# Second cross attention: ScalarE rounds the tokens, and the order of token and key work changes

## The reference

```
def _L1_xattn_ref(q, k, v, Wq, bq, Wk, bk, Wv, bv, Wo, bo):     # k = v = ctx_512, 16 heads of 8
    qh = (q @ Wq + bq).reshape(B, LQ, HEADS, D_K).transpose(0, 2, 1, 3)
    kh = (k @ Wk + bk).reshape(B, LKV, HEADS, D_K).transpose(0, 2, 1, 3)
    vh = (v @ Wv + bv).reshape(B, LKV, HEADS, D_K).transpose(0, 2, 1, 3)
    attn = jax.nn.softmax(jnp.einsum('bhqd,bhkd->bhqk', qh, kh) * scale, axis=-1)
    out = jnp.einsum('bhqk,bhkd->bhqd', attn, vh)
    return concat @ Wo + bo
```

## Time and profile before

| | us |
|---|---|
| median of 3 executions | 628.56 |
| lowest and highest | 625.13, 633.34 |
| the profiled execution's own time | 629.66 |
| span of the profiled execution | 627.8 |
| busy in the span: PE | 566.9 (90%) |
| busy: DVE | 444.7 (71%) |
| busy: POOL | 380.6 (61%) |
| busy: ACT | 372.0 (59%) |
| mean granted PE clock | 0.98 of full speed |

### The profile page before, as it was taken

One profiled execution on the slowest core, in us unless ns is written; L12 is line 12 of the kernel. 1 busy time (PEld: TensorE's weight loads), 2 busy tenths in 40 slices (PEclk: granted clock), 3 DMA queues, 4 the chain that ended last, 5 costly groups with the idle time before them and its releaser, 6 DMA issues.

```text
span 627.8 us, 18969 instructions
## 1 busy us (share of the span) xinstructions
PE 566.9 (90%) x8256; PEld 416.1 (66%) x8256; DVE 444.7 (71%) x698; ACT 372.0 (59%) x623; POOL 380.6 (61%) x271
## 2 busy tenths in 40 slices
PE   9788898899999999999888979977889889889897
PEld 4566775566767767666777556664667767778765
DVE  3876728697887887786356774776888988986543
ACT  2335674657657667566462417474677777777552
POOL 1572451488989889864630231175999999977500
PEclk9789999999999999999999999997999999999998
DMA  5830015002101101010013000412422432330000
GB/s 169 238 133 2 3 40 180 2 1 42 34 7 41 26 15 40 3 40 3 2 60 123 2 0 3 99 39 64 103 67 45 96 78 52 78 77 4 2 1 15
DMA packets 33838, 31.81 MB, mean 51 GB/s; under 512 B 27124, under 2 KB 27380, under 8 KB 33756
## 3 DMA queue, kind: packets, MB, share of 16 engines
q1 hardware_dynamic: 33756, 30.60, 18.8%
HBM read 13.06 MB, written 0.23 MB: 21 GB/s over the span
## 4 chain that ended last, share of the span: by engine, by line
PE 62%; DVE 18%; ACT 8%; issue 7%; POOL 3%; DMA 1%; DVEq 0%; POOLq 0%; ACTq 0%
PE psum L1143 9%; DVE scratch L1306 6%; PE psum L1067 5%; PE psum L1119 5%; PE psum L1503 4%; PE psum L1112 4%; PE psum L1114 4%; PE psum L1526 4%; DVE scratch L1291 4%; PE psum L217 3%; POOL scratch L1291 2%; ACT scratch L1276 2%; POOL scratch L652 1%; PE psum L1073 1%; PE psum L248 1%
## 5 line engine op out<-in xcount | busy, mean ns | idle before, releaser
L1291 POOL TENSOR_TENSOR scratch<-scratch 125x896 bf16<-125x896 f32 x143 | 242.7, 1715 | 80.4 <-ACT scratch L1276 79.9
L1306 DVE TENSOR_REDUCE scratch<-psum 128x1 f32<-128x500 f32 x336 | 210.3, 672 | 23.1 <-PE psum L1067 9.6
L1276 ACT ACTIVATE scratch<-psum 125x896 f32<-125x896 f32 x192 | 173.6, 917 | 82.8 <-PE psum L1143 51.1
L1112 PE MATMUL psum<-tok_high,scratch 125*128 125x65 bf16 x1344 | 107.0, 194 | 3.3 <-issue 2.7
L1114 PE MATMUL psum<-tok,scratch 125*128 125x64 bf16 x1344 | 106.4, 194 | 0.0
L1112 PEld LDWEIGHTS psum<-tok_high,scratch 125*128 125x128 bf16 x1344 | 94.8, 98 | 13.9 <-ACT scratch L1276 6.0
L1114 PEld LDWEIGHTS psum<-tok,scratch 125*128 125x128 bf16 x1344 | 88.6, 98 | 17.1 <-issue 0.5
L1143 PE MATMUL psum<-scratch 65*128 65x448 bf16 (+1 forms) x384 | 87.3, 352 | 0.0
L1291 DVE TENSOR_TENSOR scratch<-scratch 125x896 bf16<-125x896 f32 x49 | 67.5, 1383 | 22.8 <-ACT scratch L1276 21.1
L1119 PE MATMUL psum<-tok_high,scratch 125*128 125x65 bf16 x1344 | 72.7, 194 | 4.8 <-POOL scratch L1291 3.1
L1503 PE MATMUL psum<-scratch 128*128 128x500 bf16 x168 | 64.2, 382 | 10.8 <-DVE scratch L1306 6.5
(11 more groups left out here) (340 smaller groups left out, 870.5 us busy)
## 6 DMA issues: line engine op xcount, KB each, us to landing
nrm<-scratch SPq DMA_DIRECT2D x64, 96.0 KB, 2.2
nrm<-w_third SPq DMA_DIRECT2D x32, 96.0 KB, 2.2
raw<-ctx_dram SPq DMA_DIRECT2D x4, 672.0 KB
w_third<-fifth_dram SPq DMA_DIRECT2D x3, 595.0 KB, 6.0
w_third<-third_dram SPq DMA_DIRECT2D x2, 844.0 KB, 8.9
w_third<-third_dram SPq DMA_DIRECT2D x2, 843.5 KB, 6.8
w_fourth<-fourth_dram SPq DMA_DIRECT2D x3, 542.5 KB, 5.8
scratch<-scratch SPq DMA_DIRECT2D x8, 192.0 KB, 2.6
```

What stands on the lines that cost most here:

```text
L1112: nc.tensor.matmul(psum[:, sums, 65 * r:65 * r + 65], rows, t1[:, c, :], start=(c == 0 and r == 0), stop=False, skip_group_check=True)
L1276: nc.scalar.activation(CR["p"][0:CP, n % RING, :].rearrange("p (f n) -> p f n", f=2), psum[0:CP, S:S + 2, 0:HALF], ACT.Exp).then_inc(self. ...
L1291: ops.tensor_tensor(CR["pl"][0:CP, n % RING, :], CR["p"][0:CP, n % RING, :], p_high(n % RING), ALU.subtract).then_inc(done, 1)
L1306: nc.vector.tensor_reduce(mxp[:, r, t:t + 1], bank(B, TB), X_AXIS, ALU.max).then_inc(self.aux_freed, 1)
```

## The change

- In batches 1 to 5, ACT casts the tokens of batch b+2 (`high_tokens`, one lot after the exponential of chunk 2, one after that of chunk 4), and POOL makes both remainders behind its low part of chunk 4 (`low_tokens`, called for chunk 5). In batch 0 POOL still does all of it in chunks 1 and 2.
- DVE has the low parts of chunks 5 and 6 in place of 1 and 2, from batch 1 on. In batch 0 it keeps 1 and 2.
- In batch 0 the K units for batch 1 stand in chunks 0, 0 and 1 instead of 0, 1 and 2, its M units begin in chunk 2, and the copies of batch 1's rounded tokens (`high_act`) move from chunks 0 and 1 to 2 and 3. In batches 1 to 6 the counts of M units change.
- SP turns the tokens of batch 2 ahead of the regrouping of batch 1.
- The helpers `scale_tokens` and `tokens_pool` are split off; the first cross attention issues the same instructions in the same order.

```diff
@@ -954,7 +954,7 @@
                         "ya_in", "yb_in", "q_high", "max_set", "rec_set", "mean_set", "low_dve", "low_pool",
                         "front_act", "front_dve", "front_low"))
 
-                self.front, self.split_at, self.low_dve_at = self.plan()
+                self.front, self.low_dve_at = self.plan()
                 self.order = [(u, 0) for u in self.front]
                 self.steps = []
                 for b in range(BATCH):
@@ -973,7 +973,7 @@
 
             def plan(self):
 
-                return FRONT, (1, CHUNKS - 1), (1, 2, CHUNKS - 1)
+                return FRONT, (1, 2, CHUNKS - 1)
 
             def place(self, b):
                 return placement(b < BATCH - 1, b > 0)
@@ -1265,6 +1265,8 @@
                 if (b, c) == (0, 9):
                     context_rstd(act, 1)
 
+            second_high = (0, 1)
+
             def run_act(self, act):
                 for n in range(CHUNKS * BATCH):
                     b, c = n // CHUNKS, n % CHUNKS
@@ -1275,8 +1277,8 @@
                     S = 2 + 2 * (n % 2)
                     nc.scalar.activation(CR["p"][0:CP, n % RING, :].rearrange("p (f n) -> p f n", f=2),
                                          psum[0:CP, S:S + 2, 0:HALF], ACT.Exp).then_inc(self.probs, 1)
-                    if n in (0, 1):
-                        self.high_act(act, 1, n)
+                    if n in self.second_high:
+                        self.high_act(act, 1, n - self.second_high[0])
                     self.beside_act(act, b, c)
                     for unit in units:
                         self.act_unit(act, *unit)
@@ -1369,30 +1371,53 @@
                     projected()
 
 
+            def scale_tokens(self, pool, b, k):
+                at = slice(CHUNKS * b + 6 * k, CHUNKS * b + 6 * k + 6)
+                nc.gpsimd.tensor_tensor(nrm[:, at, :], nrm[:, at, :], bc(crstd[:, at], CD), ALU.mult
+                                        ).then_inc(tok_scaled, 1)
+
             def split_tokens(self, pool, b, k):
 
                 i, lot = b % TOKENS, slice(6 * k, 6 * k + 6)
                 at = slice(CHUNKS * b + 6 * k, CHUNKS * b + 6 * k + 6)
                 src = self.src[:, at, :]
                 if self is cross1:
-                    nc.gpsimd.tensor_tensor(src, src, bc(crstd[:, at], CD), ALU.mult).then_inc(tok_scaled, 1)
+                    self.scale_tokens(pool, b, k)
                     pool.wait_ge(tok_scaled, 2 * b + k + 1)
                 nc.gpsimd.tensor_copy(tok[i][:, lot, 64:128], src).then_inc(self.tok_high, 1)
+                self.low_tokens(pool, b, k)
+
+            def high_tokens(self, act, b, k):
+
+                at = slice(CHUNKS * b + 6 * k, CHUNKS * b + 6 * k + 6)
+                act.wait_ge(self.pv_done, CHUNKS * (b - 2))
+                if self is cross1:
+                    act.wait_ge(tok_scaled, 2 * b + k + 1)
+                nc.scalar.activation(tok[b % TOKENS][:, 6 * k:6 * k + 6, 64:128], self.src[:, at, :], ACT.Copy
+                                     ).then_inc(self.tok_high, 1)
+
+            def low_tokens(self, pool, b, k):
+                i, lot = b % TOKENS, slice(6 * k, 6 * k + 6)
                 pool.wait_ge(self.tok_high, 2 * b + k + 1)
-                nc.gpsimd.tensor_tensor(tok[i][:, lot, 0:64], src, tok[i][:, lot, 64:128],
-                                        ALU.subtract).then_inc(self.tok_set, 1)
+                nc.gpsimd.tensor_tensor(tok[i][:, lot, 0:64], self.src[:, CHUNKS * b + 6 * k:CHUNKS * b + 6 * k + 6, :],
+                                        tok[i][:, lot, 64:128], ALU.subtract).then_inc(self.tok_set, 1)
 
             def run_pool(self, pool):
                 for n in range(CHUNKS * BATCH):
                     b, c = n // CHUNKS, n % CHUNKS
                     if self.low_on_pool(n):
                         self.low_part(pool, nc.gpsimd, n, self.low_pool)
-                    if c in self.split_at and b < BATCH - 2:
-                        if b:
-                            pool.wait_ge(self.pv_done, CHUNKS * b)
-                        if self is cross1 and b == 2:
-                            pool.wait_ge(cx_rstd, 2)
-                        self.split_tokens(pool, b + 2, self.split_at.index(c))
+                    if b < BATCH - 2:
+                        self.tokens_pool(pool, b, c)
+
+            def tokens_pool(self, pool, b, c):
+
+                if c in (1, CHUNKS - 1):
+                    if b:
+                        pool.wait_ge(self.pv_done, CHUNKS * b)
+                    if b == 2:
+                        pool.wait_ge(cx_rstd, 2)
+                    self.split_tokens(pool, b + 2, int(c > 1))
 
             def turn_tokens(self, sp, b):
 
@@ -1413,7 +1438,7 @@
 
 
 
-            units_last = ()
+            units_last, second_high = (), (2, 3)
 
             def __init__(self, tag, src, wv):
                 super().__init__(tag, src, None, wv)
@@ -1421,18 +1446,18 @@
                 self.turned, self.key_in = ([sem(f"{tag}_{n}{i}") for i in range(2)] for n in ("turned", "key_in"))
 
             def plan(self):
-                return [("K", k) for k in range(3)] + FRONT[2:], (1, 2), (1, 2)
+                return [("K", k) for k in range(3)] + FRONT[2:], (5, 6)
 
             def place(self, b):
                 at = [[] for _ in range(CHUNKS)]
                 if b < BATCH - 1:
                     left = [("M", u) for u in range(21)]
-                    for c, n in enumerate((2, 1, 1, 2, 3, 3, 3, 2, 2, 1, 1) if b else (0, 0, 0, 0, 3, 3, 3, 3, 3, 3, 3)):
+                    for c, n in enumerate((2, 1, 2, 3, 3, 1, 1, 3, 2, 2, 1) if b else (0, 0, 1, 3, 3, 3, 3, 2, 2, 2, 2)):
                         at[c] += [[left.pop(0)] for _ in range(n)]
                     at[11] += [[], [("A", 0)], [("A", 1)]]
                 for c, lots in enumerate(at):
-                    if b == 0 and c < 3:
-                        lots += [[], [], [("K", c)]]
+                    if b == 0 and c < 2:
+                        lots += [[("K", 0)], [("K", 1)]] if c == 0 else [[("K", 2)]]
                     if b and c == 3:
                         lots += [[]] * (1 - len(lots)) + [[("N", 0)]]
                     if b and c == 5:
@@ -1446,6 +1471,19 @@
 
             def slot(self, h):
                 return h
+
+            def low_on_pool(self, n):
+                if n < CHUNKS:
+                    return n not in (1, 2)
+                return super().low_on_pool(n)
+
+            def tokens_pool(self, pool, b, c):
+
+                if b == 0 and c in (1, 2):
+                    self.split_tokens(pool, 2, c - 1)
+                if b and c == 5:
+                    for k in range(2):
+                        self.low_tokens(pool, b + 2, k)
 
             def keys_grouped(self, b):
                 return self.key_in[b % 2], 16 * 12 * (b // 2 + 1)
@@ -1550,6 +1588,8 @@
                         ins.then_inc(self.q_block, 1)
 
             def beside_act(self, act, b, c):
+                if b and c in (2, 4) and b < BATCH - 2:
+                    self.high_tokens(act, b + 2, c // 2 - 1)
                 if c in (7, 8) and b < BATCH - 2:
                     self.high_act(act, b + 2, c - 7)
                 if 4 <= c < 8 and b < BATCH - 1:
@@ -2283,8 +2323,10 @@
             cross2.turn_tokens(sp, 0)
             cross2.turn_tokens(sp, 1)
             for b in range(BATCH):
+                if b == 1:
+                    cross2.turn_tokens(sp, 2)
                 cross2.group_keys(sp, b)
-                if 0 < b < BATCH - 1:
+                if 1 < b < BATCH - 1:
                     cross2.turn_tokens(sp, b + 1)
             for p, cols in enumerate(HALVES):
                 sp.wait_ge(*both(ln_c, "x6")[p])
```

## The result

The changed kernel takes 647.21 us (median of 4, 641.59 to 648.82) against 629.33 before (median of four executions, where the prediction had three). The ratio is 1.0261, interval 1.0209 to 1.0313: slower, where I forecast 629.1 with a range of 620 to 637 and gave "slower by over 2%" a chance of 0.05. The profiled execution is the fastest of the four, 641.59 us with a span of 639.8, 12.0 us longer than before's. The other three took 645.9 to 648.8 us at a mean granted clock of 0.958 to 0.963, against 0.973 in the profiled one, and have no trace; that their 4 to 7 us more are clock is likely but not shown.

The account below looks back on a forecast made before the run. No engine had much to spare, so order decided: DVE's low parts early, then mostly PE. Batch 0 -5.5, steady batches +6.3, batch 6 -0.7, batch 7 +0.4 gave +0.5 us: 629.1 us for the median, range 620 to 637.

Parts of the forecast that it names:

- Batch 0: First batch of the stage: transpose ahead of the regrouping brings batch 1's first scores to 435.9 from 441.44, 5.5 us gained.
- The transpose becomes the bound of a steady batch: Batches 1 to 5: tokens' transpose lands at +15.4, so the K unit starts at +15.45 at the soonest, though PE is ready at +14.4.
- I take one lost turn: Steady batches: DVE's low parts delay POOL's subtractions by one turn of 1.0 us, K unit at +16.45; none and two as ends.
- The stretch from the K unit on: Steady batches, first K unit to next batch's first scores: 7.5 us in place of 7.31, for one more M unit.
- my 23.95 for one: Steady batch with one turn lost: 16.45 + 7.5 = 23.95 us, 1.25 more than before.
- rival 2: Steady batches: late transpose idles PE at the first K unit and halves the clock, 645 us; chance 0.05.
- POOL's relief is worth nothing by itself: Steady batches: ACT's casts relieve POOL by 2.8 us a batch, worth nothing since PE has the end of the batch.
- The landing of 3.7 us: Tokens' transpose in each batch: lands 3.7 us after its issue, as the trace shows in each of eight cases.
- Batches 6 and 7: Last two batches: batch 6 0.7 us less (0 to 1.4), batch 7 0.4 more (0 to 1).
- The ends of the sum: Whole kernel: the +0.5 us total was given -4.9 to +8.7 from the ends of its terms.

Follow-up runs that it names:

- e1: The kernel before with only SP's order changed, batch 2's tokens turned ahead of batch 1's regrouping: 627.62 us, ratio 0.9952.
- e5: The changed kernel with ScalarE's casts in chunks 2 and 3 and POOL's subtractions one low part sooner: 629.54 us, ratio 1.0006.
- e6: The changed kernel with DVE's low parts in chunks 6 and 7 in place of 5 and 6: 652.47 us, ratio 1.0353.
- e10: The kernel of e5 with DVE's low parts in chunks 4 and 5 in place of 5 and 6: 624.16 us, ratio 0.9901.
- e9: The changed kernel with the M counts of before in batches 1 to 6: 634.17 us, ratio 1.0062.
- e4: The changed kernel with 20 dummy matmuls on PE ahead of the first K unit in batches 1 to 5: 639.27 us, ratio 1.0148.
- e7: The kernel before with the change's batch 0 part and SP's order, plus ScalarE's token casts in chunks 1 and 2 of batches 1 to 5: 620.24 us, ratio 0.9861.
- e3: The changed kernel with DVE's low parts back in chunks 1 and 2 of batches 1 to 6: 661.31 us, ratio 1.0510.

## Why the prediction was wrong, point by point

- **Batch 0, right.** Predicted 5.5 us less by the transpose ahead of the regrouping, with DVE then held by the regrouping until 429.3; measured 4.8 less, DVE released at 429.08, no clock lost. e1 shows that SP's order alone brings 1.2 of it.
- **The transpose becomes the bound of a steady batch, right.** PE was to be ready at +14.4 (measured +14.2), the K unit no sooner than +15.45. e5 moves the second cast and the subtractions, and this wait is gone; e6 puts a sixth low part ahead of them, and it grows.
- **"I take one lost turn": the first step that failed.** I had both low parts on top of the subtractions and priced each turn, and took one as the middle. Two were lost, in all five batches. I had DVE's low part of chunk 5 within 0.1 us of the end of POOL's last low part and did not ask what the side means. It starts 0.10 us ahead of the first subtraction (473.22, 473.32), so that one stands; and the new counts leave one M unit between DVE's low parts, so the next starts at 474.82, before the delayed first subtraction is done, and the second stands too. e10 has the same single M unit but the low part behind the subtraction's start, and loses one turn. A turn costs 0.84 us (3.48 - 2.64), not 1.0.
- **The stretch from the K unit on, mis-sized.** 7.5 us were forecast for the extra M unit in it; 7.9 were measured, also in e10, and 7.4 in e9 with the old counts. So the order's 24.78 us against 23.95 is 0.45 for the K unit (+16.9 against +16.45) and 0.4 for this stretch, together 4.2 us in five batches. That 24.78 lies near my 24.95 for two turns, and e9's 23.94 on my 23.95 for one, is in part luck: the turn was priced too high and this stretch too low, and in e9 PE comes to the K unit 0.6 us after the landing, with the shorter stretch behind it.
- **The clock: the second step that failed, and the larger one.** I gave rival 2 a chance of 0.05, put its idle at 2.0 us with one turn lost and up to 3.0 with two, and had nothing for the clock in the forecast's sum. The idle was 2.7 us in four batches and 3.7 in one, and four of the five had half clock: 8.0 us in the profiled execution. With the clock held up (e4) some 8 us are gone. The rival's mechanism is what happened. That its time of 645 stands 2 us from the median of 647.2 is partly luck, since the execution with a trace took 641.6. Having seen that both low parts fall on the subtractions, I should have given two turns and the clock most of the chance.
- **"POOL's relief is worth nothing by itself": wrong, in another place than the change has it.** e7 shows 0.7 us a batch at chunk 2, where the cast had put POOL's first subtraction in the way of DVE's low part. In the changed kernel that low part has moved away. ScalarE's cast took 0.52 us, as forecast.
- **The landing of 3.7 us, right as a median, too narrow.** It reached 4.7 us in batch 1 of the changed kernel and 5.0 in e4. The trace of before had shown such a case outside this stage, among the first cross attention's transposes (L1402), which I had not read:

```profile
DMA to landing us min/median/max: 3.7/3.8/5.4
```

  The Trainium skill, DMA: Bandwidth & Descriptors, section "Latency and other measured facts", gives a bandwidth, from which my estimate was 1.5 us. It says nothing of the time from issue to landing, of which SP's issue alone is 1.45 us here; the trace decides.
- **Batches 6 and 7, right.** -0.7 and +0.4 were forecast. Batch 6 measured -0.8, and batch 7, from its first scores to its last product, 17.9 us against 17.5, +0.4. What follows the stage was 1.6 shorter; the kernel before has half clock there from 617.0 to 620.4 us, the changed one has not.
- **The ends of the sum, miscounted.** By its own terms they are -5.6 (-5.5 + 1.3 - 1.4) and +9.0 (-3.3 + 11.3 + 1.0), not -4.9 and +8.7. It changes nothing: +12.0 in the trace lies outside both.

What stays open: why the clock held in batch 2, whose idle of 2.7 us is as long as batch 3's; what the three executions without a trace lost; and why some transposes land a microsecond later than others.

## What to carry to other kernels

When work is moved between POOL and DVE, draw both engines' SBUF operations on one line of time: a pair that overlaps does not share, one stands for the other, and what is queued behind pays too. A unit that waits for a chain (ScalarE, POOL, SP, a landing) is to be given its margin by the rows of that chain, and the work left beside the wait is worth keeping, since here an idle of PE in one piece of 2.7 us cost its length and, in three batches of four, the clock as well. A forecast that hangs on two instructions 0.1 us apart is a forecast of two cases, and the dearer one is to be priced with all that follows from it. Where a list of placements has several parts, the parts are to be run apart: here batch 0's part with ScalarE's casts, put in chunks 1 and 2, beat the kernel before by 1.4%, and the whole lost 2.6%.

## What the runs showed of the hardware that I had not expected

- POOL and DVE exclude one another for whole instructions: two subtractions of 125x384 took 1.79 us undisturbed (e3, e5), 2.64 with one DVE low part among them (e6, e9, e10) and 3.48 with two (the changed kernel). A DVE low part of 1.08 us took 2.48 behind a POOL one (e3). DVE's maxima, which read PSUM, do not take part: one took 0.67 us in the middle of POOL's subtractions (e10, 471.00).
- The same DMA transpose landed between 3.7 and 5.0 us after its issue in one execution (e4).
- PE idles of 2.7 us, four alike in length, left the granted clock at 1.00 in one batch of the changed kernel, and in three it was halved for 3.4 to 6.8 us. With an idle of 1.9 us (e5) it was halved in two batches of five.
